# Moving each cycle's products with V from its end to its middle in an attention and LoRA layer

## The chip, the cores and the metric

The kernel runs on one core of one Trainium2 chip. The metric is the time of one execution on the device, in microseconds (us). TensorE does the matrix products, ScalarE (ACT) the exponentials and copies, VectorE (DVE) the row maxima and the residuals, GpSimd (POOL) the causal masks and small splits, SyncE (SP) issues the DMAs. Each engine works through its own instructions strictly in the order written. They meet only at semaphores.

## The reference

```python
# x: (1, 1024, 512), 32 heads of 16, 8 groups of keys and values, 4 heads to a group
q = x @ Wq;  k, v = split(x @ Wkv)
scores = einsum('bhqd,bhkd->bhqk', q, k)
scores = where(causal, -inf, scores)
ctx = einsum('bhqk,bhkd->bhqd', softmax(scores / sqrt(16)), v)
x = layernorm(x + ctx @ Wo + bo)
h = einsum('bsd,nrd->nbsr', x, lora_A)
x = layernorm(x + x @ W.T + bias + einsum('nbsr,nor->bso', h, lora_B * coef))
```

## The kernel before

The work is written out by hand, one program per engine. After an opening stage (splits of x and of the weights, the first projections), the attention runs in 80 **cycles**, numbered 0 to 79 here. The 1024 queries are two halves of 512. A unit `u` (16 of them) is one half for one group of 4 heads. A cycle `(u, s, p)` takes 256 queries (`s` = 0 or 1) of the unit against a pair `p` of key blocks (256 keys). In the first half of the queries (cycles 0 to 23) a unit has 3 cycles, in the second half (24 to 79) 7. The last cycle of each `(u, s)` is on the diagonal. It has 3 score pieces in place of 4, and its probabilities are masked by POOL (L696), one instruction per piece.

What TensorE does in a cycle, in this order:

1. Four times (`j` = 0 to 3): a lot of chunk scores (`chunk_scores`, L1128), which serve only the row maxima that DVE takes (L908, L915) for a later unit; one score piece (`piece_scores`, L1340, 128 x 512), into one of 3 banks of PSUM, or of 6 once the chunk scores have ended (from cycle 71); a part of a filler (`filler`): a projection (L1190), the transposes of a finished context (L1236, L1244), the product with Wo or the feed-forward product (L1190), the product of the LoRA matrices (L1223). Some cycles have no filler. Long fillers have a part behind every piece, short ones behind the second and the fourth.
2. The products with V of the **cycle before** (`accumulate`, L1318): 8 products in the program, which the trace shows as 16 matmuls of 32 columns of weights each, four heads side by side.
3. In 15 of the cycles (the first is 1, then 4, 7, 9, 12, 15, 18, 21, and 28 and every seventh up to 70) the maxima of a later unit are turned into rows (`turn_maxima`, L1137).

ACT does in a cycle: first, where the cycle two back was the last of its `(u, s)`, the **evacuation** of that one (`evacuate`, L770, which frees the bank of the products with V), then the exponential of each piece (L856), behind the first of them in a few cycles the scaling of a layer norm (L788), and at the end what the filler needs: copies of projections (L732, L737), the high half of a combined weight (L717) or of Wo (L809), of a turned context or norm (L776, L782), and the rows of maxima (L743).

The waits that matter here stand at the head of `accumulate` (L1305 on):

```python
if on_diagonal(cyc):
    pe.wait_ge(masked, 3 * sum(1 for c in LAST_OF if c <= cyc))
pe.wait_ge(probs, SCORE_BANKS[cyc + 1])
if p == 0 and u + s:
    pe.wait_ge(raw_out, 2 * u + s)
```

`probs` counts exponentials: all of the cycle must be done. `masked` counts POOL's masks. `raw_out` counts evacuations: the first cycle of each `(u, s)` may not write its bank before ACT has copied out the one before. `piece_scores` waits for `probs` too, for the piece that used the same bank: three pieces back, later six. ACT waits for `pv_done` of three cycles back before it writes a buffer of probabilities again (`NP_BUF = 3`). DVE's maxima have three banks (`MAX_BANKS = 3`), and the chunk scores wait for them (`max_read`).

After cycle 79 come the transposes, projections and norms of the last four blocks of rows, the tail; `accumulate(79)` stands in it as its third item.

Of the kernel before, what the change touches and what calls it, by code (L numbers as in the profile page):

```python
# [18 lines left out]

def postln_kernel(nc, x, wq, wkv, wo, bo, lora_a, lora_b, w, bias, lora_w, xt, out):  # L20
    _, T, D = x.shape
    N_LORA, RANK, _ = lora_a.shape

# [35 lines left out]
    def key_blocks(cyc):  # L59
        p = CYCLES[cyc][2]  # L60
        return 2 * p, 2 * p + 1

    def on_diagonal(cyc):
        u, s, p = CYCLES[cyc]
        return p == 2 * half_of(u) + s

    def pieces(cyc):

        first = [(0, range(0, 2), 0), (0, range(2, 4), 0)]
        return first + ([(1, range(0, 4), P)] if on_diagonal(cyc) else [(1, heads, 0) for _, heads, _ in first])  # L70
# [23 lines left out]
    def chunk_cost(ch):  # L94

        _, qb, own, heads = ch
        if not own:
            return 65 + HT
        return len(heads) * (80 + (qb + 1) * P)
# [110 lines left out]
    def chunks_of_cycle(c):  # L210

        lot = range(DUE[c], DUE[c + 1])
        return [lot[len(lot) * q // 4:len(lot) * (q + 1) // 4] for q in range(4)]
# [72 lines left out]
    with ctx:  # L286
# [129 lines left out]
        def freed(job):  # L416

            kind, b, _ = job
            if kind == "rows":
                return nm_rows, b + 1  # L420
            if kind in ("T1a", "T1b"):
                return ctx_ready, 2 * b + (2 if kind == "T1b" else 1)
            if kind in ("T2", "WO", "T3", "FF"):
                return {"T2": ct_ready, "WO": y1_read, "T3": x1t_ready, "FF": y2_read}[kind], b + 1
            if kind in BY_ACT:
                return v_read, nth(job, BY_ACT)
            return job_freed, nth(job, DVE_KINDS)
# [674 lines left out]
        def _(pe):  # L1102
# [7 lines left out]
            def chunk_scores(n):  # L1110

                u, qb, own, heads = CHUNKS[n]
                h, g = divmod(u, G)
                if n == UNIT_CHUNKS[u]:
                    if u == 0:
                        pe.wait_ge(moved_act, 1 + REP // 2)
                        pe.wait_ge(moved_dve, REP // 2)
                    else:
                        pe.wait_ge(qs_in[u % SLOTS], 48 * (u // SLOTS + (u % SLOTS > 0)))
                    if u == 1:  # L1120
                        pe.wait_ge(ks_in[0], 96)
                    if u == G:
                        pe.wait_ge(ks_in[1], 96)
                width = (qb + 1) * P if own else HT
                k0 = h * HT if own else 0
                was_read(CHUNK_BEHIND[n])
                for k, j in enumerate(heads):
                    last = nc.tensor.matmul(PS[:, CHUNK_BANK[n], k * width:(k + 1) * width],  # L1128
                                            QS[0:ROWS, u % SLOTS, j, qb * P:(qb + 1) * P],
                                            KS[0:ROWS, g, k0:k0 + width], start=True, stop=True)  # L1130
                last.then_inc(max_scores, 1)

            def turn_maxima(u):
                was_read(MISC_BEHIND["rows", u, 0])
                pe.wait_ge(nm_parts, u + 1)
                for qb in range(TB):
                    last = nc.tensor.matmul(PS[0:NPART * REP, MISC_BANK["rows", u, 0], qb * P:(qb + 1) * P],  # L1137
                                            NMP[:, u % 2, qb, :, :].rearrange("p a j -> p (a j)"),
                                            ident_bf[:, :], start=True, stop=True)
                last.then_inc(nm_turned, 1)  # L1140
# [33 lines left out]
            def rows_moved():  # L1174

                pe.wait_ge(first_row, 1)
                pe.wait_ge(nm_rows, 1)
                pe.wait_ge(odd_rows, REP // 2)
# [110 lines left out]
            def filler(cyc, head):  # L1289

                if cyc not in FILL:
                    return
                kind, b, _ = job = FILL[cyc]
                long = kind in LONG
                if not long and head % 2 == 0:
                    return
                part, parts = (head, REP) if long else (head // 2, 2)
                if job in JOB:
                    pe_job(JOB[job], part, parts)
                else:  # L1300
                    if part == 0:
                        was_read(MISC_BEHIND[job])
                    pe_step(kind, b, MISC_BANK[job], part, parts)

            def accumulate(cyc):  # L1305

                u, s, p = CYCLES[cyc]
# [3 lines that stand above are left out]
                if cyc == 0:  # L1311
                    pe.wait_ge(*freed(FIRST_BEHIND[PV_BANK]))
                if p == 0 and u + s:
                    pe.wait_ge(raw_out, 2 * u + s)
                for k, (i, heads, skip) in enumerate(pieces(cyc)):
                    width = HQ - skip
                    for n, j in enumerate(heads):
                        last = nc.tensor.matmul(PS[32 * j:32 * j + 32, PV_BANK, s * HQ + skip:(s + 1) * HQ],  # L1318
                                                VX[:, key_blocks(cyc)[i], u % G, :],
                                                PB[:, cyc % NP_BUF, k, n * width:(n + 1) * width],  # L1320
                                                start=(p == 0 and i == 0), stop=(on_diagonal(cyc) and i == 1))
                last.then_inc(pv_done, 1)

            def piece_scores(cyc, k):

                u, s, _ = CYCLES[cyc]
                i, heads, skip = pieces(cyc)[k]
                kb = key_blocks(cyc)[i]
                e = SCORE_BANKS[cyc] + k
                if e < ST_BANKS:  # L1330
                    pe.wait_ge(*freed(FIRST_BEHIND[score_bank(e)]))
                elif WIDE <= e < WIDE + MAX_BANKS:
                    pe.wait_ge(max_read, len(CHUNKS))
                elif e >= WIDE + MAX_BANKS + ST_BANKS:
                    pe.wait_ge(probs, e - MAX_BANKS - ST_BANKS + 1)
                elif e >= WIDE:
                    pe.wait_ge(probs, WIDE)
                elif e >= ST_BANKS:
                    pe.wait_ge(probs, e - ST_BANKS + 1)
                nc.tensor.matmul(PS[:, score_bank(e), :], KS[0:NROW, u % G, kb * P:(kb + 1) * P],  # L1340
                                 QS[0:NROW, u % SLOTS, heads[0]:heads[-1] + 1, s * HQ + skip:(s + 1) * HQ],
                                 start=True, stop=True).then_inc(scores, 1)

            for cyc, (u, _, _) in enumerate(CYCLES):
                if cyc == 0:
                    rows_moved()
                elif cyc == FIRST[u]:
                    pe.wait_ge(nm_in, 16 * NPART * u)
                for j, lot in enumerate(chunks_of_cycle(cyc)):
                    for n in lot:  # L1350
                        chunk_scores(n)
                    if j < len(pieces(cyc)):
                        piece_scores(cyc, j)
                    filler(cyc, j)
                if cyc:
                    accumulate(cyc - 1)
                if cyc in ROWS_AT:
                    turn_maxima(ROWS_AT[cyc])
            pe.wait_ge(max_read, len(CHUNKS))
# [62 lines left out]
```

## Time and profile before

| | us |
|---|---|
| median of 3 runs (lowest, highest) | 342.46 (341.93, 342.88) |
| profiled execution, its time | 342.48 |
| profiled execution, its span | 340.8 |
| PE busy in the span | 323.8 (95%) |
| DVE busy | 257.2 (75%) |
| ACT busy | 220.6 (65%) |
| POOL busy | 135.9 (40%) |

The span runs from the first to the last instruction that the profiler recorded; the execution's own time is 1.7 us longer. Busy time is that of the instructions as recorded. A matmul's record is longer than its share of the engine: score pieces of 0.38 us start 0.22 us after one another, so an engine may be recorded as busy without a gap and still lose up to 0.16 us between two of them. The granted clock of TensorE was 0.999 of full speed over the span.

### The profile page before, as it was taken

The numbers are of one execution on the slowest core, as the hardware profiler recorded it, in microseconds if no ns is written. First come the engines' busy times: TensorE is split into PE (matmuls) and PEld (weight loads), VectorE is DVE, ScalarE is ACT, GpSimd is POOL, SyncE is SP. The second block draws the span as 40 slices with busy tenths as digits, with TensorE's granted clock in tenths as the row PEclk, the third lists the DMA queues.
The fourth block names the chain that finished last, engine by engine and source line by source line (L and its number), as shares of the span: only waits on it lengthen the run. The fifth ranks groups of instructions, "written<-read, shape, count | busy, mean of one in ns | idle before, by whom it ended". The sixth has DMA issues, their size and how long they took to land.

```text
span 340.8 us, 7329 instructions
## 1 busy us (share of the span) xinstructions
PE 323.8 (95%) x2532; PEld 172.3 (51%) x2532; DVE 257.2 (75%) x786; ACT 220.6 (65%) x418; POOL 135.9 (40%) x268
## 2 busy tenths in 40 slices
PE   6899879999999999999999999999999999999993
PEld 2666444555444444454454444544545545458882
DVE  3647968989878889988889889888887961037664
ACT  4645637746748887757758768478587686962431
POOL 8855324423627675546122113120141122321553
PEclk9999999999999999999999999999999999999999
DMA  7785594773143111020010100000000000000002
GB/s 212 265 162 147 144 185 131 217 231 114 48 156 112 48 51 46 2 50 1 3 46 34 41 11 2 1 33 1 3 0 3 32 1 3 2 25 6 2 31 92
DMA packets 15563, 22.96 MB, mean 67 GB/s; under 512 B 1972, under 2 KB 9480, under 8 KB 15528
## 3 DMA queue, kind: packets, MB, share of 16 engines
q1 hardware_dynamic: 15528, 22.51, 23.3%
q8 instruction: 20, 0.33, 0.4%
q14 instruction: 15, 0.12, 0.1%
HBM read 16.29 MB, written 6.03 MB: 65 GB/s over the span
## 4 chain that ended last, share of the span: by engine, by line
PE 78%; DVE 8%; issue 5%; ACT 4%; DMA 3%; POOL 1%; SPq 1%; POOLq 0%; DVEq 0%; ACTq 0%
PE PS L1190 19%; PE PS L1318 19%; PE PS L1128 17%; PE PS L1340 16%; DVE scrap L915 3%; PE PS L1244 2%; PE PS L1236 2%; ACT PB L856 2%; DVE MX L908 2%; DMA X<-in_L_attn_x_turned_dram 2%; DMA QS<-NMR 1%; PE PS L1223 1%; PE PS L1145 1%; PE PS L1137 1%; ACT NMR L743 1%
## 5 line engine op out<-in xcount | busy, mean ns | idle before, releaser
L856 ACT ACTIVATE PB<-PS 128x512 f32<-128x512 f32 x288 | 155.2, 601 | 55.5 <-PE PS L1340 54.3
L915 DVE CUSTOM_DVE_ANT_0 scrap<-PS,mask 128x128 bf16<-128x128 f32 (+3 forms) x256 | 111.6, 487 | 18.4 <-PE PS L1128 17.8
L1128 PE MATMUL PS<-KS,QS 96*128 96x512 bf16 (+3 forms) x384 | 108.0, 329 | 2.2 <-DVE MX L908 0.8
L1340 PE MATMUL PS<-QS,KS 99*128 99x512 bf16 x288 | 106.5, 382 | 1.0 <-ACT PB L856 0.6
L908 DVE TENSOR_REDUCE MX<-PS 128x1 f32<-128x512 f32 x128 | 82.0, 684 | 12.0 <-PE PS L1128 11.3
L696 POOL TENSOR_SCALAR_AFFINE_SELECT PB<-PB 128x256 f32<-128x256 f32 (+1 forms) x96 | 46.4, 486 | 106.1 <-ACT PB L856 103.0
L1318 PE MATMUL PS<-PB,VX 128*32 128x256 f32 (+1 forms) x1280 | 78.8, 364 | 0.6 <-ACT PB L856 0.3
L1128 PEld LDWEIGHTS PS<-KS,QS 96*128 96x128 bf16 x384 | 32.7, 97 | 50.9 <-issue 13.0
L1318 PEld LDWEIGHTS PS<-PB,VX 128*32 128x32 f32 x1280 | 33.5, 109 | 41.8 <-issue 18.9
L1190 PE MATMUL PS<-XT,WQ 128*128 128x512 f32 x144 | 44.0, 431 | 2.2 <-DVE XT L1036 1.8
L1340 PEld LDWEIGHTS PS<-QS,KS 99*128 99x128 bf16 x288 | 27.5, 98 | 31.1 <-ACT PB L856 8.4
L1190 PEld LDWEIGHTS PS<-XT,WQ 128*128 128x128 f32 x144 | 26.2, 189 | 10.7 <-DVE XT L1036 2.2
L1190 PE MATMUL PS<-WQ,XT 128*128 128x512 f32 x96 | 28.2, 427 | 0.0
L1190 PE MATMUL PS<-XT 128*128 128x512 f32 x96 | 28.2, 427 | 0.0
L677 POOL TENSOR_SCALAR mv<-mv 128x1 f32<-128x1 f32 x15 | 3.4, 228 | 48.6 <-DVE mv L1005 48.5
L915 DVE DVE_READ_ACCUMULATOR2_ANT MX<- 128x1 f32 x256 | 21.4, 83 | 0.0
L1190 PEld LDWEIGHTS PS<-WQ,XT 128*128 128x128 f32 x96 | 17.9, 189 | 4.0
L1190 PEld LDWEIGHTS PS<-XT 128*128 128x128 f32 x96 | 18.0, 190 | 3.6
L770 ACT ACTIVATE RAW<-PS 128x256 f32<-128x256 f32 x32 | 12.3, 384 | 11.0 <-PE PS L1318 10.8
L788 ACT ACTIVATE TC<-RAW,shift,rstd 128x512 f32<-128x512 f32 x7 | 5.7, 817 | 13.4 <-POOL shift L679 13.4
L743 ACT ACTIVATE NMR<-PS 12x512 bf16<-12x512 f32 x15 | 8.8, 584 | 6.5 <-PE PS L1137 6.5
L732 ACT ACTIVATE parts<-PS 128x512 bf16<-128x512 f32 x10 | 6.0, 598 | 10.5 <-PE PS L1190 10.5
(92 smaller groups left out, 268.4 us busy)
## 6 DMA issues: line engine op xcount, KB each, us to landing
scr_q<-parts SPq DMA_DIRECT2D x8, 384.0 KB, 4.0
QS<-scr_q SPq DMA_DIRECT2D x15, 192.0 KB, 3.0
X<-in_L_attn_x_turned_dram SPq DMA_DIRECT2D x8, 256.0 KB, 6.0
X<-in_L_attn_x_dram SPq DMA_DIRECT2D x8, 256.0 KB, 3.0
out_dram<-TC SPq DMA_DIRECT2D x8, 256.0 KB, 2.0
QS<-scr_q SPq DMA_DIRECT2D x15, 128.0 KB, 3.1
RAW<-in_L_attn_Wo_dram SPq DMA_DIRECT2D x2, 512.0 KB, 5.9
RAW<-in_L_ffn_W_dram SPq DMA_DIRECT2D x2, 512.0 KB, 8.9
```

Of the source, the lines that this page charges most:

```text
L696: nc.gpsimd.affine_select(out=blk, in_=blk, compare_op=ALU.is_ge, fill=0.0, base=0, pattern=[[0, len(heads)], [1, P]], channel_multiplier=-1)\
L743: nc.scalar.activation(NMR[0:NPART * REP, u % 2, :], PS[0:NPART * REP, MISC_BANK["rows", u, 0], :], ACT.Copy)\
L770: nc.scalar.activation(RAW[:, u, cols], PS[:, PV_BANK, cols], ACT.Copy).then_inc(raw_out, 1)
L856: nc.scalar.activation(PB[:, cyc % NP_BUF, k, :], PS[:, score_bank(e), :], ACT.Exp, scale=SCALE)\
L908: nc.vector.tensor_reduce(part[:, j0:j1, 0:1], bank, AX, ALU.max).then_inc(max_read, 1)
L915: last = nc.vector.tensor_tensor_reduce(out=scrap[:, n % 2, (j - j0) * width:(j - j0 + 1) * width], in0=bank[:, j - j0, :], in1=mask[:, HT ...
L1128: last = nc.tensor.matmul(PS[:, CHUNK_BANK[n], k * width:(k + 1) * width], QS[0:ROWS, u % SLOTS, j, qb * P:(qb + 1) * P], KS[0:ROWS, g, k0 ...
L1190: last = nc.tensor.matmul(bank, lhs(a, c), rhs(b, c), start=(k == 0), stop=(k == len(terms) - 1))
L1236: last = nc.tensor.transpose(bank[:, g * P:(g + 1) * P], RAW[:, h * G + g0 + g, qb * P:(qb + 1) * P], ident[:, :])
L1244: last = nc.tensor.transpose(bank[:, c * P:(c + 1) * P], src[:, c * P:(c + 1) * P], ident[:, :])
L1318: last = nc.tensor.matmul(PS[32 * j:32 * j + 32, PV_BANK, s * HQ + skip:(s + 1) * HQ], VX[:, key_blocks(cyc)[i], u % G, :], PB[:, cyc % NP ...
L1340: nc.tensor.matmul(PS[:, score_bank(e), :], KS[0:NROW, u % G, kb * P:(kb + 1) * P], QS[0:NROW, u % SLOTS, heads[0]:heads[-1] + 1, s * HQ + ...
```

## The change

`accumulate(cyc - 1)` moves from behind all four lots to behind the second filler part of the cycle. The same instructions run. Only TensorE's order changes: 1390 lines of difference on PE, while DVE, ACT, POOL and SP have the same rows as before. The calls in the tail stay where they were.

```diff
                     if j < len(pieces(cyc)):
                         piece_scores(cyc, j)
                     filler(cyc, j)
-                if cyc:
-                    accumulate(cyc - 1)
+                    if j == 1 and cyc:
+                        accumulate(cyc - 1)
                 if cyc in ROWS_AT:
                     turn_maxima(ROWS_AT[cyc])
```

TensorE in cycle 16, from its second score piece to the first matmul of the products with V, before (L1340 with QS and KS is a score piece, L1128 a chunk score, L1223 the product of the LoRA matrices, L1318 the products with V):

```order
L1340 MATMUL PS<-QS,KS 128x512 [waits probs]
L1128 MATMUL PS<-KS,QS 128x384 [waits max_read,nm_rows]
L1340 MATMUL PS<-QS,KS 128x512 [waits probs]
L1128 MATMUL PS<-KS,QS 128x384 [waits max_read] x2
L1340 MATMUL PS<-QS,KS 128x512 [waits probs]
L1223 MATMUL PS<-TC 128x512 [waits b_scaled]
L1318 MATMUL PS<-PB,VX 32x256 [waits raw_out,probs,masked]
```

The same stretch with the change, on to the LoRA product:

```order
L1340 MATMUL PS<-QS,KS 128x512 [waits probs]
L1318 MATMUL PS<-PB,VX 32x256 [waits probs,raw_out,masked,nm_rows]
L1318 MATMUL PS<-PB,VX 32x256 x3
L1318 MATMUL PS<-PB,VX 32x128 x4
L1128 MATMUL PS<-KS,QS 128x384 [waits max_read]
L1340 MATMUL PS<-QS,KS 128x512 [waits probs]
L1128 MATMUL PS<-KS,QS 128x384 [waits max_read] x2
L1340 MATMUL PS<-QS,KS 128x512 [waits probs]
L1223 MATMUL PS<-TC 128x512 [waits b_scaled]
```

Two score pieces, three chunk scores and the LoRA product, which stood ahead of the products with V and their waits, now stand behind them.

ACT at the turn from cycle 15 to 16, the same before and with the change (L856 the exponentials of cycle 15, and behind the evacuation L770 those of cycle 16):

```order
L856 ACTIVATE PB<-PS 128x512 [waits scores] x2
L717 ACTIVATE XT<-RAW 128x512 [waits job_freed]
L737 ACTIVATE parts<-TC 128x512 [waits job_freed]
L743 ACTIVATE NMR<-PS 12x512 [waits nm_in,nm_turned]
L809 ACTIVATE WQ<-RAW 128x512 [waits job_done,wo_in]
L770 ACTIVATE RAW<-PS 128x256 [waits pv_done]
L856 ACTIVATE PB<-PS 128x512 [waits scores] x4
```

Four other ACT instructions stand between the last exponential of cycle 15 and the evacuation for which the products with V of cycle 15 wait, in either order of TensorE.

## Rows read from the trace of the kernel before

**Rows 1.** The page: busy time by engine.

```profile
PE 323.8 (95%) x2532; PEld 172.3 (51%) x2532; DVE 257.2 (75%) x786; ACT 220.6 (65%) x418; POOL 135.9 (40%) x268
```

**Rows 2.** Stretches: start:end, length, busy us of the engines, granted clock, DMA share, GB/s.

```profile
45.00:60.00 15.00, 14.68 (x110) 7.82 (x109) 12.33 (x53) 9.23 (x19) 5.64 (x13) 1.00 0.68 153
60.00:100.00 40.00, 38.67 (x302) 20.25 (x301) 33.68 (x145) 24.46 (x48) 16.70 (x37) 1.00 0.52 159
100.00:140.00 40.00, 39.15 (x353) 17.02 (x356) 36.09 (x104) 31.25 (x64) 24.45 (x42) 1.00 0.20 59
180.00:220.00 40.00, 40.00 (x345) 19.71 (x337) 34.06 (x97) 28.46 (x55) 9.82 (x24) 1.00 0.07 19
```

**Rows 3.** Who waited for whom: us in total, times, longest.

```profile
ACT PB L856 <- PE PS L1340: 54.3, 69, 2.6
ACT RAW L770 <- PE PS L1318: 10.8, 12, 1.8
PE PS L1137 <- POOL NMP L662: 1.8, 1, 1.8
```

**Rows 4.** Groups by line and form: count, busy us, mean ns, idle before.

```profile
L1318 PE MATMUL PS<-PB,VX 128*32 128x256 f32 x1024 | 71.8, 386 | 0.6 <-ACT PB L856 0.3 <-ACT RAW L770 0.2
```

**Rows 5.** Timeline, cycles 41 and 42: start, us, engine, line, operation, count.

```profile
184.97 0.38 PE L1340 MATMUL PS<-QS,KS 99*128 99x512 bf16 x1
185.28 0.86 PE L1318 MATMUL PS<-PB,VX 128*32 128x256 f32 x16
186.07 0.39 PE L1128 MATMUL PS<-KS,QS 96*128 96x512 bf16 x1
186.25 0.39 ACT L770 ACTIVATE RAW<-PS 128x256 f32<-128x256 f32 x1
...
186.73 0.38 PE L1340 MATMUL PS<-QS,KS 99*128 99x512 bf16 x1
```

**Rows 6.** Timeline, cycles 15 and 16.

```profile
101.54 1.57 ACT L856 ACTIVATE PB<-PS 128x512 f32<-128x512 f32 x3 [0.79 <-PE PS L1340]
...
101.94 0.38 PE L1340 MATMUL PS<-QS,KS 99*128 99x512 bf16 x1
...
102.16 0.38 PE L1128 MATMUL PS<-KS,QS 96*128 96x512 bf16 x1
102.21 1.61 POOL L696 TENSOR_SCALAR_AFFINE_SELECT PB<-PB 128x256 f32<-128x256 f32 x3 [1.59 <-ACT PB L856]
...
103.14 0.39 PE L1137 MATMUL PS<-ident_bf,NMP 128*12 128x128 bf16 x4
...
104.13 0.38 PE L1340 MATMUL PS<-QS,KS 99*128 99x512 bf16 x1
...
105.03 0.36 ACT L770 ACTIVATE RAW<-PS 128x256 f32<-128x256 f32 x1
```

**Rows 7.** Timeline, cycles 3 and 4, the first of its kind.

```profile
51.83 0.38 PE L1340 MATMUL PS<-QS,KS 99*128 99x512 bf16 x1
...
53.41 0.40 ACT L770 ACTIVATE RAW<-PS 128x256 f32<-128x256 f32 x1
```

**Rows 8.** Timeline, cycles 21 and 22, the last of its kind.

```profile
120.89 0.38 PE L1340 MATMUL PS<-QS,KS 99*128 99x512 bf16 x1
...
123.87 0.36 ACT L770 ACTIVATE RAW<-PS 128x256 f32<-128x256 f32 x1
```

**Rows 9.** Timeline, ACT between cycles 34 and 35.

```profile
162.56 0.59 ACT L782 ACTIVATE XT<-PS 128x512 fp32r<-128x512 f32 x1
```

**Rows 10.** Timeline, TensorE and ACT in the last ten cycles.

```profile
278.07 0.82 PE L1340 MATMUL PS<-QS,KS 99*128 99x512 bf16 x3
...
286.23 1.07 PE L1318 MATMUL PS<-PB,VX 128*32 128x256 f32 x16
...
287.72 2.07 ACT L856 ACTIVATE PB<-PS 128x512 f32<-128x512 f32 x4 [2.16 <-PE PS L1340]
288.20 0.86 PE L1318 MATMUL PS<-PB,VX 128*32 128x256 f32 x16
...
301.51 1.07 PE L1318 MATMUL PS<-PB,VX 128*32 128x256 f32 x16
...
304.27 1.97 PE L1236 MATMUL PS<-ident,RAW 128*128 128x128 f32 x16
```

**Rows 11.** Groups: the first matmuls, ahead of all others, 128 x 512.

```profile
L1269 PE MATMUL PS<-Z 128*128 128x512 bf16 x9 | 4.0, 628 | 1.2 <-DVE Z L1039 1.2
```

## The prediction

> **What bounds the kernel now.** I read the busy times first: TensorE 323.8 of 340.8 us, no other engine over 75% [rows 1]. Then the stretches: in the cycles TensorE is recorded as busy for 38.67 of 40 us, 39.15 of 40 and 40.00 of 40 [rows 2]. Then the waits: ACT waits 54.3 us for score pieces [rows 3], while the products with V, 1024 of the 1280 matmuls, saw 0.6 us without a matmul ahead of them [rows 4]. So TensorE sets the pace and ACT follows close behind. A pause of TensorE in a cycle lengthens the kernel by its own length. The products with V hardly wait because they stand a whole cycle behind the exponentials that they need. The question is what is left of that distance.
>
> **The change part by part.** Nothing is added or removed. TensorE issues the same matmuls, and the switch to 32-column weights and back happens once per cycle as before, so that moved work costs nothing by itself. It passes no DMA: those of SP and their issue order stay, and so do those of ACT, DVE and POOL. What changes is what TensorE has to do between a cycle's last score piece and the products with V of that cycle. Before, a full cycle of pieces stood there, and the products of one cycle earlier. Now it is the lots of half a cycle. The products of the cycle earlier have gone ahead of that last piece.
>
> For each of the 79 cycles I compare two times, both counted from the start of the last score piece of the cycle before.
>
> *Cover* is TensorE's own work to the end of the second piece (with its filler) of the cycle, less the products with V, which no longer lie there. Cycle 42: the last piece of 41 starts at 184.97, the second of 42 at 186.73 and takes 0.38; the products with V cost 186.07 - 184.97 - 0.22 = 0.88 of it. Cover 2.14 - 0.88 = 1.26 us [rows 5].
>
> *Chain* is what the products wait for. Piece 0.38 [rows 5]; exponential 0.60, which is what the last of a row of them takes over the 0.52 between starts; and 0.09 for the two handovers, my allowance: 1.07 us. With a mask, 0.70 more: exponentials end at 103.11, masks at 103.82 [rows 6]. That is 1.77. With an evacuation, 0.39 [rows 5] and 0.1 for one handover more, in all 1.56, and whatever else ACT has between the exponential and the evacuation.
>
> Where the chain is longer than the cover, TensorE stands for the difference. Sorted by kind:
>
> (a) Seven cycles in the first half (4, 7, 10, 13, 16, 19, 22) need an evacuation, and in front of it ACT has one to four other copies. Cycle 16: last piece at 101.94, evacuation over at 105.39 [rows 6], so 3.45 us; less the 0.16 by which that exponential was late, plus 0.1 to TensorE, 3.39. Cover: 104.13 + 0.38 - 101.94, less 103.14 - 102.16 - 0.22, is 1.81. It stands for 1.58 us, the largest. The first of them: 1.97 - 0.16 + 0.1 against 1.49, 0.41 [rows 7]. The last: 3.34 - 0.16 + 0.1 against 1.81, 1.47 [rows 8]. The seven in this way are 0.41, 0.64, 0.55, 0.84, 1.58, 0.92 and 1.47, **6.4 us**.
>
> (b) Ten cycles need an evacuation and no mask: 0.30 each in 28, 42 and 56 (1.56 against 1.26), 0.52 in 23, under 0.1 in 25, 39 and 53, and 0.67 in 35, 49 and 63, where the copy of a turned norm (0.59) stands in front [rows 9]. That is 3.6. Pieces three and four now follow the products, 0.44 us apart where ACT takes 0.52 for each (four in 2.07 [rows 10]), so add 0.08 for each: **4.2 us**. The others of the kind have a long filler or more chunk scores ahead of their middle, and enough cover.
>
> (c) Masks without an evacuation: 0.29, 0.51 and 0.23 in 18, 21 and 34, 0.07 in 48 and 62: **1.2 us**. Exponentials alone (1.07 against 1.05 to 1.7): nothing.
>
> (d) Cycles 70 to 79 have no chunk scores, so cover is short and ACT close to full. Now TensorE and ACT take turns. The products take 1.06 us with the switches; the third piece needs 0.04 + 0.42 to its exponential, two exponentials 0.52 + 0.60: 2.64 us from one group of products to the next, where 286.23 to 288.20 was 1.97 [rows 10]. From the middle of cycle 70 (278.51, the third piece started at 278.07 in its row) I go on: 1.06 to the first products (0.16 to the end of the piece, 0.90 short of the evacuation), 2.64 for cycle 70, 6.6 for 71 and 72 with the long filler, as before, 3.1 (evacuation), 3.0 (evacuation and layer norm ahead of two exponentials), 2.8 (mask), 6.6 for 76 and 77, 2.64, and 1.28 for the last products and the last piece. That ends at 308.2, against 304.27 for the first transpose of the tail [rows 10]: **4.0 us**. In the tail the last products stand behind 16 transposes (1.97 us), as long as their chain of 1.8, so nothing is added there.
>
> (e) Back comes what TensorE now stands for anyway. In 45 to 140 us it is idle 0.32 + 1.33 + 0.85 = 2.5 us [rows 2], mostly behind DVE's maxima, which catch up while TensorE stands elsewhere: **-2.5 us**, between 0 and -3.6. In cycle 1 it waits 1.8 us for POOL ahead of the turned maxima [rows 3], with or without the products in front: nothing.
>
> Sum: 6.4 + 4.2 + 1.2 + 4.0 - 2.5 = 13.3 us. Bounds of the unknowns: (a) falls to 4 if the copies ahead of the evacuation have caught up, since ACT is idle for part of each pause; (d) lies between 2 and 5.5. The profiled execution took 342.48 us, the median of the runs is 342.46. **Forecast 355.8 us**, +3.9%. A measurement of this kernel can tell about 0.3%, 1 us, from no change.
>
> A clock of TensorE at its lower level would be dearer. Before, it was granted 1.00 in every one of these stretches [rows 2], while the first 128 x 512 matmuls, at the lower one of 1.2 and 2.4 GHz, took 628 ns [rows 11] against 0.38 us later. The Trainium skill, "TensorE: Matmul & The Clock Gate", section "A second HAM failure mode: psum-queue depth-cycling", says that short idles between groups of matmuls that wait for PSUM can make the clock swing between its levels. By it the sum would not hold. The rows don't bear it out: TensorE stood 1.33 us of 40 in short pauses already, at full clock [rows 2].
>
> **The rivals.**
>
> *Only half of it comes through*, 24%: 349 us. DVE is recorded as busy for 36.09 of 40 us from 100 to 140 [rows 2]. If there the maxima and not TensorE set the pace, (a) is covered in good part: 6.4 falls to 2, and (d) to 2: 342.5 + 2 + 3.6 + 1 + 2 - 2.5 = 348.6. For it: the waits for the maxima in that half. Against it: those leave TensorE only 0.85 us idle in 40.
>
> *The pauses pass on*, 12%: 362 us. While TensorE stands in (a), DVE gets no chunk score and starves after its three banks, so that the maxima come late, too, and the rows of maxima after them. At 0.9 us for each of seven cycles more it is 342.5 + 13.3 + 6.3 = 362. Against it: in the first half each pause is shorter than the 2 us of work in three banks.
>
> *Not slower*, 7%: 341.5 us. Evacuations get their products half a cycle earlier: ACT waits 10.8 us for them in 12 waits [rows 3]. If ACT's lag and not a fixed chain sets when the exponentials end, the earlier evacuation pulls the exponentials forward, TensorE finds everything ready, and its idle time of 2.5 us shrinks instead: 342.5 - 1 = 341.5. It decides where the chain is shorter than the cover in (a), 1.8 us: there ACT would have to reach the evacuation 0.8 us after the exponential, where it now takes 2.28 in cycle 16 (103.11 to 105.39, [rows 6]).
>
> *The clock swings*, 2%. If the last ten cycles (26 us) ran at half the clock, TensorE's 25 us in them doubled: 342.5 + 13 + 25 = 380.
>
> **How the numbers follow.** My own case has 55%, at 352 to 359. The predicted time is its 355.8. The range must leave out no more than two in ten: it reaches from 347, under the half case at 349 and its bounds, to 361, at the lower part of the passing case. Slower by over 0.3%: 0.55 + 0.24 + 0.12 + 0.02, 0.93. Of the 7% not slower, 4 lie within 0.3% and 3 below.
>
> **What would show it.** Idle time ahead of L1318 grows from 0.6 us to several, put down to ACT's L770 and L856 and POOL's L696. Cycle 16's products start about 1.5 us behind the end of its second piece. Groups of products in the last cycles stand 2.6 us apart, and the first transpose of the tail starts some 13 us later than 304.27, 9 of them gained before cycle 70. ACT's total waiting for score pieces grows by about 10 us. The granted clock stays at 1.00. The prediction is wrong if L1318 does not wait, if the pauses in the first half are under 3 us in all, or if the tail, from 304.27 to the end, becomes longer.

## The result and the profile after

The change made the kernel slower: 362.75 us median of 4 runs (361.64 to 363.03) against 342.67 (341.93 to 343.73), a ratio of 1.058 with a 95% interval of 1.055 to 1.061. The forecast had the sign and the place of most of it, at 355.8; 362.75 lies 1.8 us above its range. The profiled execution after took 363.03 us, its span 361.3.

The page after, busy time by engine:

```profile
PE 331.9 (92%) x2532; PEld 175.0 (48%) x2532; DVE 257.0 (71%) x786; ACT 220.5 (61%) x418; POOL 135.4 (37%) x268
```

The same work on DVE and ACT as in [rows 1]. TensorE stands longer, and it is recorded as busy for 8.1 us more with the same matmuls. The groups of the products with V by form, and of the turned maxima, after:

```profile
L1318 PE MATMUL PS<-PB,VX 128*32 128x256 f32 x1024 | 72.3, 388 | 14.6 <-ACT RAW L770 10.5 <-POOL PB L696 2.2 <-ACT PB L856 0.8
L1137 PE MATMUL PS<-ident_bf,NMP 128*12 128x128 bf16 x60 | 5.9, 221 | 1.9 <-POOL NMP L662 1.8
```

0.6 us of standing ahead of the products has become 14.6 [rows 4], 10.5 of it for ACT's evacuation. Who waited for whom, after (L743 is ACT's copy of the turned maxima, PEld TensorE's loading of weights):

```profile
ACT PB L856 <- PE PS L1340: 88.7, 104, 1.9
ACT RAW L770 <- PE PS L1318: 1.3, 1, 1.3
PEld PS L1318 <- ACT NMR L743: 5.1, 4, 2.0
```

ACT waits 34.4 us longer for score pieces and 9.5 us less for the products ahead of an evacuation [rows 3]. The two have changed places: now TensorE waits for the evacuation, and in four cycles its weight loads wait for the copy of the turned maxima. The forecast had ACT's waiting for score pieces grow by about 10 us. Cycle 16 after (start, us, engine, line, operation, count):

```profile
107.27 0.38 PE L1340 MATMUL PS<-QS,KS 99*128 99x512 bf16 x1
...
108.17 0.61 ACT L809 ACTIVATE WQ<-RAW 128x512 fp32r<-128x512 f32 x1
...
108.69 0.36 ACT L770 ACTIVATE RAW<-PS 128x256 f32<-128x256 f32 x1
...
109.19 1.51 PE L1318 MATMUL PS<-PB,VX 128*32 128x256 f32 x16 [1.55 <-ACT RAW L770]
```

The second score piece ends at 107.65, the products start at 109.19: 1.55 us, where the forecast had 1.58. The group itself then took 1.51, where one of the same kind has 0.86 in [rows 5], and the stretches show why (start:end, length, busy us of PE, PEld, DVE, ACT, POOL, granted clock, DMA share, GB/s):

```profile
44.40:47.80 3.40, 3.40 (x15) 1.84 (x11) 1.11 (x5) 1.45 (x3) 0.41 (x1) 0.50 1.09 145
47.80:109.20 61.40, 56.51 (x454) 29.18 (x454) 49.18 (x207) 37.14 (x74) 25.10 (x56) 1.00 0.48 140
109.20:112.60 3.40, 3.40 (x21) 1.56 (x22) 1.16 (x2) 1.40 (x3) 2.28 (x2) 0.50 0.37 108
```

Twice in the cycles TensorE ran at 1.2 in place of 2.4 GHz for 3.4 us: behind a wait of 1.8 us for POOL in cycle 1, and behind this pause. (Both profiles also end at the lower clock, in the last 0.6 us before and 2.9 us after, in the tail, which did not become longer by it.)

**A ledger by cycles.** I subtract the length of each cycle, from its first score piece to that of the next, before from after. A *pause* is the time by which the first product starts later than right behind the matmul ahead of it; it also counts the up to 0.16 us that a record can hide. Up to the first transpose of the tail, which started at 304.27 [rows 10], after stands 20.5 us behind:

| | us | forecast |
|---|---|---|
| pauses, cycles 4, 7, 10, 13, 16, 19, 22 (a) | 6.1 | 6.4 |
| pauses, evacuation without a mask (b) | 4.0 | 4.2 |
| pauses, masks or exponentials alone, to cycle 69 (c) | 3.1 | 1.2 |
| pauses, cycles 70 to 79 (3.9, less 0.8 that were there) (d) | 3.1 | 4.0 |
| ten cycles that turn maxima, 0.22 each | 2.2 | none |
| other waits of TensorE that grew: for DVE in 66, 67, 69 (fillers: 0.72, 0.56, 0.55) and 38, 52 (chunk scores, 0.23 each), for L743 in 29, 43, 57 (fillers, 0.21 each) | 2.9 | none |
| lower clock, in cycles 2 and 16 | 1.9 | none |
| smaller differences, longer by (cycles 1, 4, 11) | 0.5 | none |
| other waits, shorter by (e): what remains to 20.5 | -3.3 | -2.5 |

### The profile page after: what moved, and what is told of

Its sections match the earlier page's. It is cut to its first block, busy times and chain, and to the rows that moved or that the text cites. A ratio compares the mean times of both kernels' runs of the same rounds, so it can differ in the third digit from the quotient of the medians.

```text
span 361.3 us, 7329 instructions
## 1 busy us (share of the span) xinstructions
PE 331.9 (92%) x2532; PEld 175.0 (48%) x2532; DVE 257.0 (71%) x786; ACT 220.5 (61%) x418; POOL 135.4 (37%) x268
## 4 chain that ended last, share of the span: by engine, by line
PE 65%; ACT 13%; issue 9%; DVE 7%; POOL 4%; DMA 1%; POOLq 0%; DVEq 0%; ACTq 0%
PE PS L1190 19%; PE PS L1318 18%; PE PS L1128 12%; PE PS L1340 10%; ACT PB L856 7%; POOL PB L696 3%; DVE scrap L915 2%; PE PS L1244 2%; PE PS L1236 1%; ACT NMR L743 1%; DVE MX L908 1%; ACT RAW L770 1%; PE PS L1145 1%; ACT parts L737 1%; DMA TC<-in_L_attn_Wkv_dram 1%
## 5 line engine op out<-in xcount | busy, mean ns | idle before, releaser
L856 ACT ACTIVATE PB<-PS 128x512 f32<-128x512 f32 x288 | 160.2, 597 | 90.7 <-PE PS L1340 88.7
L1128 PE MATMUL PS<-KS,QS 96*128 96x512 bf16 (+3 forms) x384 | 106.9, 333 | 1.8 <-DVE MX L908 1.1
L1340 PE MATMUL PS<-QS,KS 99*128 99x512 bf16 x288 | 106.9, 384 | 0.0
L908 DVE TENSOR_REDUCE MX<-PS 128x1 f32<-128x512 f32 x128 | 82.9, 685 | 22.3 <-PE PS L1128 21.8
L1318 PE MATMUL PS<-PB,VX 128*32 128x256 f32 (+1 forms) x1280 | 79.5, 366 | 14.6 <-ACT RAW L770 10.5
L1318 PEld LDWEIGHTS PS<-PB,VX 128*32 128x32 f32 x1280 | 35.1, 109 | 55.9 <-ACT PB L856 18.7
L1128 PEld LDWEIGHTS PS<-KS,QS 96*128 96x128 bf16 x384 | 33.4, 98 | 56.2 <-issue 19.4
L1190 PE MATMUL PS<-XT,WQ 128*128 128x512 f32 x144 | 46.4, 453 | 1.0 <-DVE XT L1036 0.5
L1340 PEld LDWEIGHTS PS<-QS,KS 99*128 99x128 bf16 x288 | 27.6, 98 | 24.2 <-issue 5.9
L1190 PEld LDWEIGHTS PS<-XT,WQ 128*128 128x128 f32 x144 | 27.7, 202 | 10.3 <-ACT NMR L743 1.8
L788 ACT ACTIVATE TC<-RAW,shift,rstd 128x512 f32<-128x512 f32 x7 | 5.7, 816 | 13.5 <-POOL shift L679 13.5
L770 ACT ACTIVATE RAW<-PS 128x256 f32<-128x256 f32 x32 | 12.1, 377 | 1.3 <-PE PS L1318 1.3
L1244 PE MATMUL PS<-ident,TC 128*128 128x128 f32 x64 | 11.2, 278 | 1.0 <-DVE MX L908 0.7
```

Source lines behind the costliest of these rows:

```text
L770: nc.scalar.activation(RAW[:, u, cols], PS[:, PV_BANK, cols], ACT.Copy).then_inc(raw_out, 1)
L788: nc.scalar.activation(result, Y(n), ACT.Identity, bias=shift[:, s], scale=rstd[:, s]) .then_inc(ready, 1)
L856: nc.scalar.activation(PB[:, cyc % NP_BUF, k, :], PS[:, score_bank(e), :], ACT.Exp, scale=SCALE)\
L908: nc.vector.tensor_reduce(part[:, j0:j1, 0:1], bank, AX, ALU.max).then_inc(max_read, 1)
L1190: last = nc.tensor.matmul(bank, lhs(a, c), rhs(b, c), start=(k == 0), stop=(k == len(terms) - 1))
L1244: last = nc.tensor.transpose(bank[:, c * P:(c + 1) * P], src[:, c * P:(c + 1) * P], ident[:, :])
```

## The experiments

All are variants of the line that places `accumulate`, or of ACT's order. Each ratio is to runs of the kernel before on the same chip, 343.1 to 343.4 us median there.

**early_evac**: ACT evacuates right behind the last exponential, ahead of the copies.

```diff
-                if cyc - 2 in LAST_OF:
-                    evacuate(*LAST_OF[cyc - 2])
                 for k in range(len(pieces(cyc))):
...
+                if cyc - 1 in LAST_OF:
+                    evacuate(*LAST_OF[cyc - 1])
                 kind, b, _ = job = FILL.get(cyc, ("", 0, 0))
```

> The changed kernel, with ACT's evacuation L770 moved from behind the copies at a cycle's end to ahead of them, right behind the last exponential. Fixed chains: the evacuation was the end of the chain in the seven cycles of the first half (pauses 6.1 us in the changed trace) and behind the copies of cycles 34, 48, 62 and 69; with it early only masks and exponentials are left there, the pauses ahead of L1318 fall from 17.0 to about 9 us, and the time from 362.7 to about 354. Rival, that ACT's total work and not its order holds TensorE: what the evacuation gains the delayed copies lose again, 361 to 363.

Measured 357.78 us, 1.042 (1.041 to 1.044): 5 us back, pauses 17.0 to 11.8, more than the 9 expected. Cycle 16 there:

```profile
106.83 0.38 ACT L770 ACTIVATE RAW<-PS 128x256 f32<-128x256 f32 x1
...
108.13 0.57 ACT L743 ACTIVATE NMR<-PS 12x512 bf16<-12x512 f32 x1
...
108.76 0.86 PE L1318 MATMUL PS<-PB,VX 128*32 128x256 f32 x16 [0.94 <-ACT NMR L743]
```

The evacuation is 2 us early, and now the copy of the turned maxima is late: the filler that stands ahead of the products asks for its bank. The group takes 0.86 again, and the clock did not fall here, which is about 0.9 of the 5 us. 354 us had been expected.

**rows_first_b** moves that copy forward as well.

```diff
                 if cyc - 1 in LAST_OF:
                     evacuate(*LAST_OF[cyc - 1])
+                if cyc in ROWS_AT:
+                    turn_rows(ROWS_AT[cyc])
```

> As early_evac, and ACT's copy of the turned maxima L743 is moved ahead of the other copies, too. In early_evac the products of cycles 10, 13, 16 and 19 waited for L743 (0.49, 0.79 and 1.01 us in three of them), because the filler in front of them needs the bank that it frees. With it early only masks remain: 2 us less than early_evac, 355.8. If the order of ACT's copies does not matter there: 357.8.

Measured 355.62 us, 1.036 (1.032 to 1.041), where 355.8 was expected. Pauses in the first half fall from 7.6 to 4.3 to 2.0 us over the three kernels. The seven cycles of (a) together are 5.2 us longer than before in the changed kernel, and 0.5 here. ACT's order at the cycle's end was the price of (a), and its total work was not. One part only moved: cycles 4 and 7 are still 0.93 and 1.11 us longer, with pauses of 0.36 and 0.16, for now the turn at their end waits for the late maxima:

```profile
56.17 0.38 PE L1137 MATMUL PS<-ident_bf,NMP 128*12 128x128 bf16 x4 [0.49 <-POOL NMP L662]
...
69.69 0.38 PE L1137 MATMUL PS<-ident_bf,NMP 128*12 128x128 bf16 x4 [0.92 <-POOL NMP L662]
```

**turn_apart** separates the turn of the maxima from the products in 15 cycles and leaves all else as before.

```diff
-                    if j == 1 and cyc:
+                    if cyc and j == (2 if cyc in ROWS_AT else 3):
                         accumulate(cyc - 1)
```

> The kernel before, but in the 15 cycles that turn maxima the products with V stand behind the third lot instead of the fourth, so that the turn (L1137) no longer follows them directly. If the turn needs a switch of TensorE of its own as soon as it does not follow the products, about 0.2 us in each: 3.1 us, plus 2.2 us of pauses that are left of those of the changed kernel: 347.9. If the turn costs the same anywhere: pauses alone, 344.9.

Measured 346.25 us, 1.008 (1.007 to 1.010), between the two. The trace settles it: no pause is left that before did not have (0.8 us in both), so the 2.2 us expected of pauses were wrong, and each of ten turning cycles is longer by 0.22. Cycle 35 before:

```profile
164.29 0.38 PE L1340 MATMUL PS<-QS,KS 99*128 99x512 bf16 x1
164.60 1.07 PE L1318 MATMUL PS<-PB,VX 128*32 128x256 f32 x16
165.49 0.39 PE L1137 MATMUL PS<-ident_bf,NMP 128*12 128x128 bf16 x4
165.81 0.39 PE L1128 MATMUL PS<-KS,QS 96*128 96x512 bf16 x1
```

From the start of the products to that of the turn 0.89 us, where a chunk score or piece starts 1.00 behind them (286.23 in [rows 10], the next score piece at 287.23); and after a score piece the turn starts 0.31 behind in the changed kernel, where another score starts 0.22 behind. 0.11 and 0.09 make the 0.2. I read it as a switch between 128 and fewer columns of weights, which the product group and the 12-column turn share when they stand side by side. What in the shapes costs the time was not tried apart.

**turn_kept**, the reverse: the changed kernel, with the products back at the end in the turning cycles (`j == (3 if cyc in ROWS_AT else 1)`).

> The changed kernel, but in the 15 cycles that turn maxima the products with V are back at the end, ahead of the turn. Pauses of these cycles (6.5 us) go, and those of the cycles behind them (4.9), which have a group of products in their cover again. With a switch of the turn's own, 3.1 us more: 348. Without it: 351.5.

Measured 356.17 us, 1.038 (1.036 to 1.039). Pauses fell to 8.7 us, but it gained only 6.6 us of the 11 to 15 expected. Cycles with their group back at the end, and without a pause, are still longer: 1.17 us in cycle 7, 0.57 in 35, 49 and 63, 0.77 in 70. In each of them six lots now follow one another without a group of products in between.

**quiet_b** places the products in the middle in the 38 cycles that had neither pause nor turn (a list of cycles in the same line).

> The kernel before, with the products in the middle in the 38 cycles in which the changed trace has no pause and which turn no maxima. By fixed chains and the turn's switch nothing is left to pay: 343, within 1 us of before. If moving the products costs something in itself (late maxima, uneven work for ACT), it shows here: half of the cycles, so 2 us or more.

Measured 353.46 us, 1.030 (1.026 to 1.034), 10 us and against my expectation, with 1.5 us of pauses, 0.8 of which were there before. So there is a second cost that is no pause ahead of the products. The profile of it, cycle 27, whose group stands at the end while that of 26 stood in the middle:

```profile
142.31 0.25 DVE L973 RECIPROCAL rec<-PS 128x16 f32<-128x16 f32 x1
...
142.59 0.42 DVE L974 TENSOR_TENSOR TC<-PS,rec 128x256 f32<-128x256 f32 x1
...
142.93 0.68 DVE L915 CUSTOM_DVE_ANT_0 scrap<-PS,mask 128x512 bf16<-128x512 f32 x1
...
143.54 0.68 DVE L915 CUSTOM_DVE_ANT_0 scrap<-PS,mask 128x512 bf16<-128x512 f32 x1
...
143.68 0.39 PE L1128 MATMUL PS<-KS,QS 96*128 96x512 bf16 x1 [0.62 <-DVE MX L915]
```

TensorE has run out of banks for chunk scores: six lots in 0.44 us each, and DVE needs 0.61 for each (142.93 to 143.54) and has put the scaling of a context (L973, L974), 0.62 us, in between. Cycles 27, 41 and 55 are 0.81 us longer, 39 and 53 0.48. Cycle 7 is 1.17 longer, 0.69 of it a wait of the turn for the late maxima, and 70 is 0.77 longer, where a score piece waits 0.86 us for ACT's exponentials. The group of products is what lets DVE and ACT catch up; uneven distances between groups cost even where every wait of the group itself is met.

**late_fill** is the same question for the changed kernel's own waiting fillers: middle in 66, 67 and 69 alone.

> The kernel before, with the products in the middle in cycles 66, 67 and 69 alone. In the changed trace these three are 0.72, 0.56 and 0.55 us longer without a pause ahead of the products: the filler's transposes wait for a bank that DVE still reads. If that comes from the group of products which left the end of the cycle before, and which had given DVE time, then cycle 66 is as before (the group at the end of 65 stays), 67 is about 0.5 us longer (its group went to the middle of 66), 68 is as before or a little longer, and 69 is as before (the group at the end of 68 stays). If it comes from the group's own new place in the cycle: all three longer, +1.8 us.

Measured 344.59 us, 1.004 (1.002 to 1.006). Cycles 66 and 69 are as before, 67 is 0.55 longer, 68 as before, and 70 is 0.77 longer, which I had not expected (six lots without a group, from the middle of 69 to the end of 70; a score piece waits 0.86 us for ACT's exponentials, not for DVE). In the changed kernel, cycle 66:

```profile
282.32 0.38 PE L1340 MATMUL PS<-QS,KS 99*128 99x512 bf16 x1
283.21 0.44 PE L1236 MATMUL PS<-ident,RAW 128*128 128x128 f32 x2 [0.51 <-DVE TC L1028]
```

The transposes follow 0.89 us behind the piece in place of 0.22, for DVE. The group that left the end of the cycle before had covered DVE's residual at the start of this one.

**seven_b**: middle in cycles 4, 7, 10, 13, 16, 19 and 22 alone.

> The kernel before, with the products in the middle in cycles 4, 7, 10, 13, 16, 19 and 22 alone. If the cover lost is both what stands behind the products now and the group of products of the cycle before, which here keeps its old place in front, each pause is 0.8 us shorter than in the changed kernel: 1.3 us of pauses for the 6.1 there, 344.5 to 346. If each placing costs its own pause whatever the neighbours do: 6 us, 349.

Measured 343.22 us, 1.000 (0.998 to 1.002), better than either case of the expectation. The trace has 2.95 us of pauses in these cycles, 0.16 to 1.09 in five of them, and yet cycle 16 is only 0.39 us longer and 13 is 0.59 shorter. In these cycles other waits gave back as much. It shows that the seven pauses come from two removals together, of what stands behind and of the group in front, and that this half takes up some 3 us.

**last_ten**: middle in cycles 70 to 79 alone.

> The kernel before, with the products in the middle in cycles 70 to 79 alone. By the pauses of the changed trace (3.9 us there, less 1.0 that cycle 70 keeps off and 0.8 that were there before, and 0.2 for one turn) +2.3: 345.0. By the forecast's taking turns of TensorE and ACT, +4.0: 346.7.

Measured 345.08 us, 1.005 (1.004 to 1.007), +2.0 as expected from the pauses. The forecast's 4.0 for (d) is too much.

**third_lot_b**: products behind the third lot in all cycles.

> The products behind the third lot in every cycle, halfway back. Cover grows by a chunk score and a piece, 0.44 us (0.22 in the last ten cycles), and each pause of the changed trace shrinks by that: 17.0 to about 6.3, of which 0.8 were there before; the turns' own switches stay, 2.4 us: 351 to 352. If the cost goes with the distance moved in proportion: half, 353. If the turn's switch is not real: 348.5.

Measured 349.77 us, 1.018 (1.014 to 1.022), less than expected. Pauses are 4.3 us, not 6.3; the turning cycles keep their 0.22, and cycles 66, 67 and 69 lose 0.71, 0.40 and 0.39. Two thirds of the cost go with half of the way back: each pause is what its chain is longer than its cover, so the cost does not go with the distance.

**paired, five_pairs_b, eight_pairs_b**: three kernels that try to use the shared switch. From the kernel before, the products of some cycles are held back and join the next group.

```diff
-                if cyc:
-                    accumulate(cyc - 1)
+                if cyc and cyc - 1 not in HELD:
+                    if cyc - 2 in HELD:
+                        accumulate(cyc - 2)
+                    accumulate(cyc - 1)
```

`HELD` stands for the list of cycles that is written out there. It is 25, 28, 32, 35 and so on to 63 (12 cycles) in the first, (28, 35, 42, 49, 56) in the second, and these with 31, 45 and 59 in the third.

> From the kernel before, a try to gain by the switch that turn_apart showed: in 12 places of cycles 24 to 64 the products of a cycle are held back and follow directly in one group with those of the next, at the end of a cycle. Each merging saves one switch to narrow weights and back, 0.2 us: -2.4 us, 340.7, if DVE and ACT keep up over the eight lots without a group in between. If they don't (quiet lost 0.8 us in each of cycles 27, 41 and 55, where six lots stood in a row), +0.3 to +0.8 in each place: 345 to 350.

Measured 344.97 us, 1.006 (1.003 to 1.008): a loss. By cycles, the joins behind 28, 35, 42, 49 and 56 gained 0.25 us each (1.10 less, 0.85 more), those behind 25, 32 and their like lost 0.68 and 0.47. In cycle 27 a chunk score waits 0.62 us for DVE; in cycle 34 TensorE waits 0.2 us each for ACT's exponentials and for DVE.

> The kernel before, with the products of cycles 28, 35, 42, 49 and 56 alone held back one cycle and joined to the next group. In paired these joins gave 0.25 us each (1.10 saved, 0.85 paid) and cycles 38 and 52 were 0.41 shorter: -2.1 us, so 0.994 of before. If those gains lived on the time lost elsewhere in paired (pauses in which DVE and ACT caught up), they go with it: 1.000.

Measured 341.18 us, 0.993 (0.991 to 0.996), as expected. It is faster than both kernels. The joined group (start, us, engine, line, operation, count):

```profile
146.03 0.38 PE L1128 MATMUL PS<-KS,QS 96*128 96x256 bf16 x2
146.34 1.93 PE L1318 MATMUL PS<-PB,VX 128*32 128x256 f32 x32
```

32 matmuls in 1.93 us, against 2 x 1.07. Cycles 38 and 52, whose start the double group of cycle 37 or 51 now precedes, are 0.41 shorter. That fits the mechanism of late_fill, used the other way: a longer break in front of DVE's residual.

> As five_pairs, and cycles 31, 45 and 59 are held back, too, and joined at the end of 33, 47 and 61. Three more switches saved, 0.25 us each, if DVE keeps up behind the long filler of 31: -2.8 us, 0.992. If it doesn't, +0.5 or more in each: 0.998 to 1.000.

Measured 341.31 us, 0.993 (0.991 to 0.996): the three more joins gave 0.84 to 0.87 and cost 0.97 each, so they lose 0.1 each. The expectation had DVE as what may fall behind there. It is ACT: in cycles 33, 47 and 61 the weight loads of three score pieces in a row wait for its exponentials.

## Why the prediction was right and wrong

*Chain against cover* was right. The pauses came where it had put them and in their size: 0.54, 0.88, 0.59, 0.88, 1.62, 0.49 and 1.10 us in the seven cycles of (a) against 0.41, 0.64, 0.55, 0.84, 1.58, 0.92 and 1.47, and 0.30 and 0.74 in those of (b) against 0.38 and 0.75. early_evac and rows_first_b show that ACT's order makes the chain. The four parts (a) to (d) add up to 16.3 us measured and 15.8 forecast. That the two sums lie so close is in part luck, for the errors within them cancel: single pauses of (a) are too low by up to 0.24 us and too high by up to 0.43. (c) was too low by 1.9: masks make cycles 24, 27, 41 and 55 pause by 0.15, and exponentials alone 33, 47 and 61 by 0.17, where I had nothing, and 34 has 0.73 for 0.23, since ACT takes a layer norm (L788, 0.82 us) among the exponentials of cycle 33; (d) was too high by 0.9, since I had the long chain in every cycle.

*"That moved work costs nothing by itself"* is the step that failed first. I counted the switches of the products and not the turn's, which had stood next to them in 15 cycles. turn_apart: 0.22 us in ten cycles, 2.2 us.

*"Back comes what TensorE now stands for anyway"*, -2.5, was near in size (3.3 back, as a remainder) and wrong as the whole story of DVE. I asked what the group of products waits for, and not who used its time. It stood at the end of a cycle, just ahead of DVE's residuals, and its 0.8 us was DVE's chance to catch up. Moved half a cycle forward, it left TensorE waiting elsewhere: 2.3 us for DVE and 0.6 for ACT's copy of the turned maxima, and 0.5 of smaller differences. late_fill shows it without one new pause, quiet_b with 0.7 us of them. This term and the turn's, 5.1 us, carry most of the 6.8 us by which the measured 20.1 exceed the 13.3 of the sum.

*The clock.* The rival had it falling over the last ten cycles at 2%. It fell elsewhere, for 3.4 us at a time, about 1 us each. The first fall, at 44 us, is no work of the change: kernels whose cycles up to there are the same as before have it in some runs. It was absent from the profile of before, where the stretch from 44.4 to 47.8 was granted 1.00, and present in that of last_ten. Of the 14 profiles eight have it, 0.1 to 1.9 us behind the end of that wait of 1.8 us, which all 14 have; a ninth, quiet_b, fell in the opening instead, at 7.5 us and for 6.8 us. The ten runs of last_ten split: four from 343.6 to 344.1 us at a clock of 0.996 and over, six from 345.1 to 345.6 at 0.994 and under. The second, at 109.2 us, was in the profile of the changed kernel alone, behind its longest pause, and the one of its runs with a clock of 0.994 in place of 0.987 was the fastest, 361.64. With cycle 16's pause at 1.18 us (turn_kept) or less, the profiles show no second fall. That the pause caused it was not tried by itself. The Trainium skill ("TensorE: Matmul & The Clock Gate", section "A second HAM failure mode: psum-queue depth-cycling") reports a clock that goes back and forth where TensorE idles briefly and often between groups of matmuls. This trace has 35 pauses ahead of products and one fall among them, behind the longest; the other 34 passed at full clock.

*The rivals.* "Only half comes through" named the right stretch: seven_b shows that the first half gives back what three microseconds of pauses take. "The pauses pass on" had the right total, 362, by luck, and in the main the wrong cause: not starved maxima, but the turn's own switch, fillers and chunk scores that wait for DVE and ACT because these no longer have their break, and the clock.

*The signs.* The pauses, cycle 16's 1.55 us and the groups 2.6 us apart in the last short cycles (2.57 twice) came as said. Three did not: TensorE was 17.7 us behind at the start of cycle 70 and not 9, ACT waited 34.4 us longer for score pieces and not 10, and the granted clock did not stay at 1.00.

The tail, from the first transpose to the end, stayed as long as before: 36.5 us in both.

## What to carry over

Before a group of work is moved on the engine that sets the pace, count three things: the chain behind its own waits against the work that is left as cover, including every moved neighbour; who was using its time as a break, since the engines behind it need breaks in front of their heaviest work; and what it shared with its neighbours, here 0.22 us with each turn. A pause between two groups of matmuls costs its length only where nobody else was late anyway. A ledger by cycles separates these at 0.1 us, where the total hides them.

## What the runs showed of the hardware

A turn with 12 columns of weights directly behind products with 32 columns cost 0.22 us less than the two apart (turn_apart, ten cycles), and two groups of such products joined cost 0.25 us less than two separate ones (five_pairs_b, five places). In some runs of one and the same kernel TensorE's clock dropped to its lower level for 3.4 us and came back; the six of the ten runs of last_ten with the lower mean clock took 1.5 us longer, by the medians, than the other four.
